# Audio tower kernel: shared expert's weights in a buffer of their own, the last group's routing later, two up tiles before the block's end

## Reference, cut to what matters

```
h = tok(x)            # 32 clips: frames -> 256 -> 256, relu, batch norm; 93 positions per clip
h = h + attn(layernorm(h))    # 16 heads of 64, softmax(q k^T * scale) v, then WO (1024 x 256)
z = layernorm(h)
shared = gelu(z @ shared_up) @ shared_down          # 256 -> 1024 -> 256, for every row
probs  = softmax(z @ router_w)                      # 8 experts, the best 2 of each row
routed = sum over the two of prob * (gelu(z @ up[e]) @ down[e])
out = h + shared + routed + z
```

## Time and profile before

| what | us |
|---|---|
| median of 3 runs | 1092.68 |
| profiled execution: its own time | 1093.34 |
| its span, first to last instruction | 1091.7 |
| TensorE matmul busy in it | 1030.6 (94%) |
| VectorE busy | 620.3 (57%) |
| ScalarE busy | 509.6 (47%) |
| GpSimd busy | 422.1 (39%) |
| block 2 | about 90.3 to 620.3 |
| block 3 | about 620.3 to 1091.7 |

### The profile page before, as it was taken

One profiled execution on the slowest core, in us unless ns is written; L12 is line 12 of the kernel. 1 busy time (PEld: TensorE's weight loads), 2 busy tenths in 40 slices (PEclk: granted clock), 3 DMA queues, 4 the chain that ended last, 5 costly groups with the idle time before them and its releaser, 6 DMA issues. The chain is left out here.

```text
span 1091.7 us, 24219 instructions
## 1 busy us (share of the span) xinstructions
PE 1030.6 (94%) x8364; PEld 958.2 (88%) x8365; DVE 620.3 (57%) x1610; ACT 509.6 (47%) x1129; POOL 422.1 (39%) x535
## 2 busy tenths in 40 slices
PE   5995999999999999999999899999999999999798
PEld 5994888888888888888888798999999999999798
DVE  3665666766777676777766755433333444354364
ACT  3552445444544544454444463545444455544252
POOL 2001232344342533425242330606660656164882
PEclk9996999999999999999999599999999999999899
DMA  9616999800000100001011243322333413313553
GB/s 190 127 41 217 356 345 345 281 19 24 22 23 28 28 28 15 13 29 27 28 26 61 79 137 127 111 94 94 110 113 117 134 58 134 120 44 92 137 153 99
DMA packets 104628, 115.32 MB, mean 106 GB/s; under 512 B 29856, under 2 KB 94848, under 8 KB 104576
## 3 DMA queue, kind: packets, MB, share of 16 engines
q1 hardware_dynamic: 75936, 73.82, 22.1%
q0 software_dynamic: 18176, 29.12, 9.3%
q10 hardware_dynamic: 10464, 11.70, 3.2%
HBM read 51.53 MB, written 62.95 MB: 105 GB/s over the span
## 5 line engine op out<-in xcount | busy, mean ns | idle before, releaser
L1296 POOL TENSOR_TENSOR prob<-prob,rc 93x372 f32<-93x372 f32 x128 | 103.2, 806 | 308.1 <-DVE rc L1175 307.6
L1851 DVE TENSOR_TENSOR act_s<-up_ps,act_s 128x384 fp32r<-128x384 f32 (+1 forms) x168 | 81.7, 492 | 177.1 <-ACT up_ps L1698 175.9
L908 PE MATMUL pj_ps<-xg,wA 128*128 128x372 f32 x768 | 152.7, 346 | 5.5 <-DVE split L744 3.6
L1696 ACT ACTIVATE act_s<-up_ps 128x384 fp32r<-128x384 f32 (+1 forms) x168 | 73.8, 439 | 149.3 <-PE up_ps L1589 144.8
L908 PEld LDWEIGHTS pj_ps<-xg,wA 128*128 128x128 f32 x768 | 129.4, 190 | 14.5 <-DVE split L744 4.7
L1069 ACT ACTIVATE probT<-t_ps 93x372 f32<-93x372 f32 x128 | 60.7, 474 | 93.0 <-PE t_ps L929 92.5
L894 PE MATMUL pj_ps<-wB,xg 128*93 128x512 f32 x384 | 102.7, 403 | 0.8 <-ACT h_s L666 0.8
L1179 DVE TENSOR_TENSOR oT<-o_ps,oT 128x372 fp32r<-128x372 f32 x64 | 34.8, 543 | 106.0 <-ACT oT L1074 106.0
L1589 PE MATMUL up_ps<-rx,wB 128*128 128x256 f32 (+1 forms) x576 | 86.4, 308 | 0.6 <-issue 0.6
L1603 PE MATMUL dn_ps<-wB,act_s 128*128 128x256 f32 x720 | 85.5, 279 | 0.0
L1589 PEld LDWEIGHTS up_ps<-rx,wB 128*128 128x128 f32 x576 | 83.5, 188 | 1.6 <-issue 0.8
(11 more groups left out here) (201 smaller groups left out, 1969.4 us busy)
## 6 DMA issues: line engine op xcount, KB each, us to landing
slots<-zeros SPq DMA_DIRECT2D x8, 3072.0 KB, 23.7
y_rows<-zeros SPq DMA_DIRECT2D x5, 2688.0 KB, 20.0
rows_in<-slots SPq DMA_DIRECT2D x22, 384.0 KB, 3.5
y_rows<-rows_out ACTq DMA_DIRECT2D x22, 384.0 KB, 2.5
raw<-in_L_ffn_routed_up POOLq DMA_DIRECT2D x7, 1024.0 KB, 5.5
raw<-in_L_ffn_routed_down POOLq DMA_DIRECT2D x7, 1024.0 KB, 8.1
ln_out<-split SPq DMA_DIRECT2D x8, 744.0 KB, 3.2
frames<-in_x SPq DMA_DIRECT2D x8, 400.0 KB
```

The costliest lines, as they stand in the source:

```text
L908: ins = pe.matmul(pj_ps[:, t, 0:N], wA[:, wp, at:at + P], xg[:, dp, m, :], start=(k == 0), stop=(k == 5))
L1296: pool.tensor_tensor(p, p, rc[:, u % 2, :].unsqueeze(2).broadcast_to([TP, 4, SL]), ALU.mult).then_inc(scaled, 1)
L1696: act.activation(act_s[:, HI, f, 0:width], up_ps[:, f % 4, 0:width], ACT.Gelu).then_inc(ract_hi, 1)
L1851: dve.tensor_tensor(act_s[:, LO, f, 0:width], up_ps[:, f % 4, 0:width], act_s[:, HI, f, 0:width], ALU.subtract).then_inc(ract_lo, 1)
```

## The change

1. A buffer `wS` holds the split shared weights for the rest of the kernel. POOL fills it in attention group 0: after each of the 16 scale operations, one part of 512 columns, HI at even units and LO at odd ones. `shared_hi` and `shared_lo` are gone from ACT and DVE in the last group and in `drain`.
2. In the last group the routing of group 6 stops after step 12. The steps index, expert, masks, both follow in `drain` after `take_o(6)`, and rank, pick and slots after `take_o(7)`. PE's `rank_tile` moves from step 15 to `drain`, ahead of `output(7)`.
3. The two banks of `s_ps` become `sc_ps`, which lives on in block 3 beside `up2_ps`. After `output(7)`, still in block 2, PE computes up tiles 0 and 1 of the shared expert for group 0 into `sc_ps`; block 3 begins with tile 2.
4. ACT ends block 2 with a Gelu of one column (`warm`), which brings its table load with it.
5. The experts' buffers change places, (`wA`, `wB`). The second fetch of the shared weights is gone, with PE's wait for it, and the fetch of expert 1 no longer waits for the shared work.

The diff's pieces stand in the order buffers, then block 2 on PE, ACT, DVE and POOL, then block 3.

```diff
+        wS = sb(ctx, "wS", [P, 2, 4096], F32R)
+        warm = sb(ctx, "warm", [P, 1])
+        sc_ps = ps(ctx, "sc_ps", [P, 2, 512])
-            zeros = sb(c, "zeros", [P, 2 * HD], F32R)
-            s_ps = ps(c, "s_ps", [TP, 2, 512])
+            zeros = sb(c, "zeros", [P, HD], F32R)
+            s_ps = sc_ps[0:TP, :, :]
+            def shared_up(pe, to, f):
+                k = 0
+                for m in range(MC):
+                    for wp, dp in PASSES:
+                        at = m * F + f * P
+                        ins = pe.matmul(to, wS[:, wp, at:at + P], sx[:, dp, m, :], start=(k == 0), stop=(k == 5))
+                        k += 1
+                ins.then_inc(up_done, 1)
...
-                        if s == NU - 1 and behind:
+                        if s == NU - 1 and behind and ahead:
                             rank_tile(pe, g, g - 1)
...
                     output(g, NJ - 2)
                     values(g, NJ - 1)
+                    rank_tile(pe, g, g - 1)
                     output(g, NJ - 1)
+                    pe.wait_ge(sx_in, 16)
+                    pe.wait_ge(sh_lo, SH_PARTS)
+                    pe.wait_ge(shifted, NG * NU)
+                    for f in range(2):
+                        shared_up(pe, sc_ps[:, f, 0:N], f)
...
-                        if not ahead and s >= 13:
-                            shared_hi(s - 13)
...
-                    shared_hi(3)
                     take_turned(g, NU - 1)
                     take_o(g, NJ - 1)
+                    act.activation(warm[:, :], zero_c[:, :], ACT.Gelu).then_inc(warmed, 1)
...
+                    if not ahead and s > 12:
+                        return
...
-                        if not ahead and s >= 14:
-                            shared_lo(s - 14)
...
                     take_o(g, NJ - 2)
-                    shared_lo(2)
-                    shared_lo(3)
+                    for step in ("index", "expert", "masks", "both"):
+                        route(dve, g - 1, step)
                     take_o(g, NJ - 1)
+                    take_ranks(dve, g, g - 1)
+                    route(dve, g - 1, "pick")
+                    route(dve, g - 1, "slots")
                     add(g)
...
+                def shared_part(q, low):
+                    cols = slice(q * 512, (q + 1) * 512)
+                    if not low:
+                        pool.wait_ge(raw2_in, 32)
+                        pool.tensor_tensor(wS[:, HI, cols], raw2[:, cols], zero_c[:, 0:1].broadcast_to([P, 512]), ALU.add
+                                           ).then_inc(sh_hi, 1)
+                    else:
+                        pool.wait_ge(sh_hi, q + 1)
+                        pool.tensor_tensor(wS[:, LO, cols], raw2[:, cols], wS[:, HI, cols], ALU.subtract).then_inc(sh_lo, 1)
...
+                        if not behind:
+                            shared_part(*divmod(u, 2))
...
-            up_ps = ps(c, "up_ps", [P, 4, 512])
+            up2_ps = ps(c, "up2_ps", [P, 2, 512])
-            weights = (wB, wA)
+            weights = (wA, wB)
+            def up_bank(f, width):
+                return (sc_ps if f % 4 < 2 else up2_ps)[:, f % 2, 0:width]
...
-                    if isinstance(n, int) and n == 1:
-                        pool.wait_ge(dn_done, G1 * C)
-                    else:
+                    if not (isinstance(n, int) and n == 1):
...
-                fetch(E, 0, sh_up[0].rearrange("(c p) n -> p c n", p=P), sh_down[0].rearrange("(c p) n -> p c n", p=P))
...
-                up(wA, 0, range(0, 5))
+                up(wS, 0, range(2, 5))
...
-                pe.wait_ge(w_split, E + 1)
```

More of the change, by code:

```diff
@@ L527, in audio_tower_kernel @@
         sh_hi = sem(ctx, "sh_hi")
+        sh_lo = sem(ctx, "sh_lo")
+        up_done = sem(ctx, "up_done")
+        warmed = sem(ctx, "warmed")
         sx_in = sem(ctx, "sx_in")
@@ L534, in audio_tower_kernel @@
             VW = 4 * P
+            SH_PARTS = 8
             xg = sb(c, "xg", [P, 2, MC, N], F32R)
@@ L1179, in take_o, with routing @@
                     dve.tensor_tensor(oT[:, j % 2, LO, :], o_ps[:, 0:N], oT[:, j % 2, HI, :], ALU.subtract).then_inc(o_lo, 1)
-                def routing(s, place, n):
+                def routing(s, place, n, ahead):
+                    if not ahead and s > 12:
+                        return
                     plan = {11: ("max", "shift", ""), 12: ("sum", "recip", "scale top"), 13: ("index", "expert", "masks both"),
@@ L1192, in group @@
                             shift(g, s)
-                        if s == NU - 1 and behind:
+                        if s == NU - 1 and behind and ahead:
                             take_ranks(dve, g, g - 1)
                         if behind:
-                            routing(s, 0, g - 1)
+                            routing(s, 0, g - 1, ahead)
                         if s >= 1:
@@ L1203, in group @@
                         if behind:
-                            routing(s, 1, g - 1)
+                            routing(s, 1, g - 1, ahead)
                         if s == 13 and ahead:
@@ L1235, in group @@
                                 take_logits(dve, g, g - 1)
-                            routing(s, 2, g - 1)
-                        if not ahead and s >= 14:
-                            shared_lo(s - 14)
[L1240 to L1244, removed]
+                            routing(s, 2, g - 1, ahead)
                 def start():
@@ L1365, in audio_tower_kernel @@
             v_chain = sem(c, "t_chain")
-            up_done = sem(c, "up_done")
             gelu_done = sem(c, "gelu_done")
@@ L1606, in tile @@
                     ins.then_inc(rdn_done, 1)
-                up(wA, 0, range(0, 5))
+                up(wS, 0, range(2, 5))
                 back_tile(pe, LG, 1, 1, LN, z_rows)
                 back_tile(pe, LG, 1, 0, LN, z_rows)
-                up(wA, 0, range(5, 7))
+                up(wS, 0, range(5, 7))
                 logits_tile(pe, LG, LN)
-                up(wA, 0, range(7, FC))
-                down(wA, 0, range(0, 1))
+                up(wS, 0, range(7, FC))
+                down(wS, 0, range(0, 1))
                 rank_tile(pe, LG, LN)
[L1617 to L1621, removed]
+                down(wS, 0, range(1, C))
+                up(wS, 1)
+                down(wS, 1)
+                up(wS, 2)
+                down(wS, 2, range(0, 2))
                 pe.wait_ge(taken[0], number(LG, "rank"))
@@ L1624, in _ @@
                 turn_rows(0)
-                down(wA, 2, range(2, C))
+                down(wS, 2, range(2, C))
                 pe.wait_ge(x_lo, 1)
@@ L1654, in gelus @@
                             act.wait_ge(dn_done, g * C)
-                        act.activation(act_s[:, HI, f, 0:N], up_ps[:, f % 4, 0:N], ACT.Gelu).then_inc(act_hi, 1)
+                        act.activation(act_s[:, HI, f, 0:N], up_bank(f, N), ACT.Gelu).then_inc(act_hi, 1)
                         act.wait_ge(act_hi, g * FC + (f + 1))
-                        act.activation(up_ps[:, f % 4, 0:N], up_ps[:, f % 4, 0:N], ACT.Gelu).then_inc(gelu_done, 1)
+                        act.activation(up_bank(f, N), up_bank(f, N), ACT.Gelu).then_inc(gelu_done, 1)
                 def take_x(n0):
@@ L1665, in w0_part @@
                     cols = slice(q * 1024, (q + 1) * 1024)
-                    act.activation(wB[:, HI, cols], raw[:, cols], ACT.Copy).then_inc(w0_hi, 1)
+                    act.activation(wA[:, HI, cols], raw[:, cols], ACT.Copy).then_inc(w0_hi, 1)
                 gelus(0, range(0, 5))
@@ L1695, in tile @@
                             act.wait_ge(rdn_done, 1 + n0)
-                        act.activation(act_s[:, HI, f, 0:width], up_ps[:, f % 4, 0:width], ACT.Gelu).then_inc(ract_hi, 1)
+                        act.activation(act_s[:, HI, f, 0:width], up_bank(f, width), ACT.Gelu).then_inc(ract_hi, 1)
                         act.wait_ge(ract_hi, n0 * FC + (f + 1))
-                        act.activation(up_ps[:, f % 4, 0:width], up_ps[:, f % 4, 0:width], ACT.Gelu).then_inc(rgelu_done, 1)
+                        act.activation(up_bank(f, width), up_bank(f, width), ACT.Gelu).then_inc(rgelu_done, 1)
                         if f == 4:
```

18 lines of the change are left out of this document (9 added, 9 removed).

## The result

| kernel | median of 20 runs, us | range | ratio, 95% interval |
|---|---|---|---|
| before | 1092.82 | 1092.06 to 1094.3 | |
| after | 1093.85 | 1092.22 to 1098.6 | 1.0013, 1.0007 to 1.0019 |

No gain: about 1 us slower, where 3.2 us less was forecast. The executions of the changed kernel are spread over 6.4 us here, those of before over 2.2; in a later set of 29 executions the kernel before ran from 1088.9 to 1094.5.

What follows compares the result with a forecast made beforehand. It took DVE's queue, not PE, to bound the end of block 2, with the clock falling in PE's waits; -5.0 + 1.6 + 0.2 = -3.2 us gave 1089.5 us against the median, range 1087.6 to 1094.8.

Steps and rivals of the forecast that it cites:

- the same distance from there to the end: After block 3's clock fall: an expected profile sign that the rest of the kernel takes as long as before.
- the sum behind it: Whole kernel: -5.0 + 1.6 + 0.2 = -3.2 us, giving 1089.5 us against the median.
- Parts 1 and 2: Last group without splits and late routing: output(7) ends 6.1 us earlier at full clock, 2.0 if the clock falls.
- the first rival: Last group: the clock falls all the same, output(7) ends at 617.0, total 1095.2 us; chance 0.28.
- Part 3: Two up tiles ahead: DVE starts block 3 5.0 us earlier, not 6.0; PE's 4.4 us gap drops the clock, +1.6.
- the logits' term: Block 3: logits start 0.8 to 2.3 us later relative to DVE's start; +1.6 taken.
- its +1.0 and +1.6: Block 3: DVE's start gains 5.0 us where 6.0 without the two tiles; logits then 1.6 us later.
- Part 4: End of block 2: ACT's 1.28 us table load lies under output(7) and is worth 0; 1.3 if its cover is gone.
- POOL in group 0: Attention group 0: 16 added POOL operations, 17.2 us in all, cost +0.2 us; bounds 0 and 4.8.
- the third rival: Group 0: POOL and DVE collide, costing 4.8 us instead of 0.2, total 1094.1 us; chance 0.12.
- Part 5: Routed experts: dropping the second shared-weight fetch and freeing expert 1's fetch is worth 0 for both.
- The second rival: Block 3: the gap does no harm to the clock, -5.1 us, total 1087.6 us; chance 0.10.

Runs made afterwards that it cites:

- b_shifted: The kernel before with an unused one-column buffer (32 bytes) ahead of `z_rows`, nothing of the change in it: 1097.48 us, ratio 1.0053.
- j_rx_192: a_aligned with 192 unused bytes directly ahead of `rx`: 1090.13 us, ratio 0.9976.
- a_aligned: The changed kernel with `warm` 16 columns wide instead of 1, so everything allocated after it starts 32 bytes further on: 1093.92 us, ratio 1.0021.
- i_split_first_192: d_split_first with 192 unused bytes directly ahead of `rx`: 1085.61 us, ratio 0.9950.
- c_no_ahead: a_aligned without the two up tiles at the end of block 2; block 3 begins with tile 0 again: 1090.97 us, ratio 0.9987.
- d_split_first: a_aligned with DVE's first two splits of block 3 moved earlier into the layer norm and up tile 5 ahead of the turns: 1090.47 us, ratio 0.9988.
- h_split_first_64: d_split_first with 64 unused bytes directly ahead of `rx`: 1087.86 us, ratio 0.9965.

## Why the prediction was wrong, step by step

**The failed step.** It is the sentence "the same distance from there to the end", and the sum behind it, which has no term for the buffers that the change adds. `wS` moves what follows it by a multiple of 256 bytes and is harmless; the column `warm` moves it by 32 more. That put the routed tiles at a distance of 96 instead of 64, and the 21 tiles cost 6.4 us. b_shifted shows the size without any other edit (T +6.5, in time +0.53%), j_rx_192 shows the changed kernel with the distance restored: 1090.13, ratio 0.9976, 2.6 us below before (1.4 to 3.8), where -3.2 was forecast. Otherwise the sum held; two of its terms were off in opposite directions (last group 0.5 better, logits 0.6 worse), and that they cancel is luck.

**Parts 1 and 2, the last group: right.** Forecast 6.1 us at the full clock; output(4) to the end of output(7) went from 19.91 to 13.30, 6.6. The clock stayed at 1.00, by the thin margin that the prediction named: j_rx_192, whose code in block 2 is that of a_aligned, shows the first rival in its profiled execution. Its busy table:

```profile
600.00:604.00 4.00, 2.62 (x29) 2.04 (x28) 3.64 (x9) 1.79 (x5) 1.61 (x2) 0.94 0.00 0
604.00:608.00 4.00, 4.00 (x30) 3.62 (x29) 0.96 (x4) 0.85 (x2) 1.61 (x2) 0.50 0.00 0
...
612.00:616.00 4.00, 3.76 (x25) 3.46 (x23) 1.43 (x8) 1.97 (x3) 0.00 (x0) 0.50 0.00 0
```

and its PE:

```profile
603.69 2.28 PE L971 MATMUL y_ps<-wB,oT 128*124 128x256 f32 x9 [0.23 <-DVE oT L1193]
...
614.07 2.28 PE L971 MATMUL y_ps<-wB,oT 128*124 128x256 f32 x9 [0.24 <-DVE oT L1193]
```

Output(7) ends at 616.35 there, 2.6 us before that of the kernel before, where the rival's walk had 2.0, and DVE's block 3 begins 1.2 us earlier (rival: 0.7 later). From output(4) to the end of output(7) it is 17.23 us, against 13.3 in the seven other traces of kernels with parts 1 and 2: the fall costs 3.9 us there. This execution, 1092.62, was the slowest of j's twelve. The rival is real, in one of eight profiled executions and not as the rule.

The prediction's last sentence, that executions could differ by several us, fits. For executions without a trace only the mean granted clock is on record, and it points the same way: 0.978 in the longest of the changed kernel (1098.6) and 0.983 to 0.987 in the others, 0.981 in i's two long ones and 0.984 to 0.989 in its others. But this is no mark of the changed kernel alone: before ranged over 5.6 us in the set with a_aligned, a_aligned itself over 2.6. How much of the 6.6 us came from the weights' splits and how much from the routing was not separated.

**Part 3: right in mechanism, 0.6 us short in size.** DVE's start after output(7) +1.0 as forecast. The gap was 4.22 us (forecast 4.4), and the clock fell at 618.3 (forecast 620 to 623, with a start of DVE 2.1 us later than it was) until 625.1, 6.8 us (forecast 3 to 7). Up group 1 came 2.2 us later relative to DVE's start, within the 0.8 to 2.3 of the logits' term; +1.6 was taken. (Before, the logits began 10.46 us after DVE's start, at 630.95, and not 10.55; the sum does not change by it.) c_no_ahead shows what the part cost: about 3 us (1.0 at DVE's start and 2.1 behind it), since without it PE has tiles 0 and 1 left for the time in which it now waits. The forecast has this loss too, in its +1.0 and +1.6.

The Trainium skill (TensorE: Matmul & The Clock Gate, section "Why this matters for your kernels") warns of idle gaps between bursts. The fall in the 4.2 us gap of after agrees. The length of a gap alone does not tell, though: before, a 1.4 us gap in thinly loaded work preceded a fall, and after the same 2.06 us gap the clock fell in d_split_first (0.50 from about 620.7) and stayed at 1.00 in h_split_first_64 and i_split_first_192.

**Part 4:** the table load cost nothing visible, as forecast; it was not tested by itself.

**POOL in group 0: nothing, as forecast within 0.2.** The parts of `wS`, by tile (shortest, median and longest in ns, then first and last start):

```profile
L1308 POOL TENSOR_TENSOR wS<-raw,zero_c x8: 1033/1037/1041, 110.2 to 159.1; 128x512 fp32r<-128x512 f32 x8
L1312 POOL TENSOR_TENSOR wS<-raw,wS x8: 1277/1280/1286, 114.0 to 162.6; 128x512 fp32r<-128x512 f32 x8
```

8 x 1.04 + 8 x 1.28 = 18.5 us (17.2 estimated). From group 0's first matmul to output(4) of the last group it is 498.42 us against 499.22 before. In all 14 traces it is 498.6 to 499.2 without these operations and 498.4 to 499.3 with them, so the 0.8 is not an effect of the change, and the third rival, +4.8 by collisions, is refuted. The other 0.7 us of the first line of the table lie ahead of group 0, in block 1, whose work the change leaves alone: group 0 starts at 98.3 to 99.9 us in the 14 traces.

**Part 5: right about the waits.** No wait on a fetch took the place of the one removed. The 1.2 us at the end were seen in one execution, and the last stretch takes 99.7 to 101.5 us in the traces of before and its padded copies and 99.6 to 102.2 in those of the changed kernel and its variants. In the profiled execution of after the slowest gather of the routed rows landed 8.6 us after its issue (8.0 before), and PE's longest wait for `act_s` there was 6.7 us against 4.0. Why this execution is the longest is open.

**The second rival** (gap harmless, 1087.6) fell with the clock at 618.3.

## What to carry to other kernels

Where a change adds or removes a buffer, compare the start addresses of what is allocated behind it, and measure pads of 32 to 192 bytes as experiments of their own: here a buffer of one column cost more than the change had gained. If a stretch that the change does not touch takes longer with the same waits and the same granted clock, look at the time of a single instruction in it before looking for a cause in the schedule. And work moved out of a stretch can open a gap where it was: two tiles ahead lost 3 us until the splits that PE would wait for were moved ahead as well, and even then gained at most 0.5 us over leaving the tiles where they were.

## What the runs showed of the hardware

- The pace of the routed tiles' fp32r matmuls depends on the distance, modulo 256 bytes, between the starts of activations and weights in a partition. At 64, 256 columns take mostly 113 to 114 ns (mean about 115) and 384 columns 173.4; at 96, 256 columns take 118.5 in `down` and 120 in `up`, 384 columns 176.6. Four distances were tried (64, 96, 128, 192). Why this is so is open. In a routed tile every slice keeps the distance (rows of 1536 bytes, chunks of 512); the shared expert's rows of 1488 bytes and chunks of 496 run through several distances within a tile. That would fit its steady pace, but was not tested, and nothing was tried for attention.
- The same code can keep the full clock through a thinly loaded stretch in one execution and lose it in the next (a_aligned: 1.00 through 600 to 616; j_rx_192: 0.50 from 603.5), at a price of 3.9 us between output(4) and the end of output(7). The same holds after a gap: 1.00 in h_split_first_64 and i_split_first_192, 0.50 from about 620.7 in d_split_first, 1.9 us up to group 1.
